# VectorE's scaling of a group of four tiles stands one tile later in the output projection stage

## The chip, the cores and the metric

The kernel runs on one core of a Trainium2 chip. The metric is the time of one execution on the device, in microseconds (us). Three executions of the kernel before gave 2685.3, 2689.87 and 2693.89 us, with the median at 2689.87 us.

## The reference

The reference is one transformer layer on 4096 tokens of width 512, with a context of 3202 rows. Cross attention with 16 heads is followed by a residual addition, then a mixture of 8 experts of which each token uses the best two, then another residual addition:

```python
x = x + _L0_xattn_ref(_layernorm(x), ctx, ctx, Wq, bq, Wk, bk, Wv, bv, Wo, bo)
x = x + _L0_ffn_ref(_layernorm(x), W_experts, b_experts, W_router, b_router)
# in _L0_xattn_ref, at its end:   return out @ Wo + bo
# in _L0_ffn_ref:
router_weights = jax.nn.softmax(jnp.einsum('bsd,ed->bse', x, W_router) + b_router, axis=-1)
topk_w, topk_idx = jax.lax.top_k(router_weights, 2)      # other experts get weight 0
expert_out = jnp.einsum('bsd,eod->bseo', x, W_experts) + b_experts
return jnp.einsum('bseo,bse->bso', expert_out, router_weights)
```

The change touches the part in the middle: `out @ Wo + bo`, the residual sum, the second layernorm's statistics, and the routing.

## The kernel before

The kernel has four stages, each a block of its own: `projections` (q, k, v), `attention` (the bulk of the time), `route_tokens` (the stage that is changed) and `mix_experts`. A stage begins when every engine has ended the one before. Engines run their instructions strictly in the order in which they are written; between engines the order is made by semaphores, all written out by hand.

`route_tokens` (L1172) walks over 32 tiles of 128 tokens, in eight groups of four (`G4 = 4`; below, q is the group and i the step). Per tile it does this:

- TensorE `project(i)` (L1434): 12 matmuls (L1441), attention output times Wo, split in a high and a low part, into one of four PSUM banks.
- VectorE `residual(i)` (L1357): adds x (with the bias, which GpSimd has added in `with_bias`, L1290) into `rows` (L1364), then takes the statistics (L1366).
- At a group's last tile VectorE does `spread(q)` (L1368): mean and variance of four tiles. ScalarE does `root(q)` (L1311): logarithm, then exponential, which gives 1/sqrt(variance), with a table load in front of each. VectorE does `scale(q)` (L1377): five small operations that refine it and write the scale and shift columns of `rows`; the last one raises `rows_ready`.
- ScalarE `normal(i)` (L1317, waits for `rows_ready` of its group), TensorE `turn(i)` (L1444, four transposes, L1449), ScalarE `copy_turned(i)` (L1326), TensorE `route(i)` (L1452, the router's matmuls, L1458).
- Per group VectorE does `choose(q)` (L1386, the two best experts and their counts), ScalarE `exps(q)` (L1332), VectorE `weights(q)` (L1407).

Beside this, each of the 32 steps readies one piece (128x512) of the expert weights: SyncE loads it (`load_piece`, two buffers), ScalarE rounds it (`split_high`, L1309), and VectorE (even pieces) or GpSimd (odd pieces) takes the rest (`split_low`, L1245), after which the buffer may be loaded again. SyncE issues all transfers of the stage: x tiles (`load_x`, ring of three, waits for the residual), attention output (`load_o`, 2 x 512 KB every second tile), pieces, and `store_rows(q)` (L1261), which waits for `rows_ready` and writes 1040 KB.

The order on every engine is set by constants at the head: an operation for tile n stands in step n + constant. Each engine's loop over steps then lists what stands in a step and in which order. In the kernel before, VectorE's step 4q+3 holds the residual of that tile, `spread(q)`, `weights(q-2)` and `scale(q)`; `choose(q-2)` stands in step 4q+2. ScalarE's `root(q)` stands at the end of step 4q+3, `normal(4q)` in step 4q+4. TensorE's `turn(4q)` stands in step 4q+5, behind `project(4q+5)`.

Of the kernel before, what the change touches and what calls it, by code (L numbers as in the profile page):

```python
# [1171 lines left out]
def route_tokens(nc, mem, sb0, sem, psum, ident, g, h):  # L1172
# [3 lines left out]
    NTL, K, table, we_hi, we_lo, picked, before, mix = (h[n] for n in "NTL K table we_hi we_lo picked before mix".split())  # L1176
    lane, number, own, token, rows_stored = (h[n] for n in "lane number own token rows_stored".split())
    G4 = 4
    NGR = NTL // G4
    TURN, ROUTE = 5, 6  # L1180
    NORM = 4
    FIRST_STEP, SECOND_STEP = 10, 11
    STEPS = (NGR - 1) * G4 + SECOND_STEP + 1
    WO_BANKS, T_BANK, R_BANK = 4, 4, 6
    RING = 3
# [1 line left out]
    with mem:  # L1187
# [48 lines left out]
        def piece(n):  # L1236
            return n % KT, n // KT

        def lo_of_piece(eng, n):
            return eng.wait_ge(we_lo_pool, n // 2 + 1) if n % 2 else eng.wait_ge(we_lo_dve, n // 2 + 1)  # L1240

        def split_low(eng, n, done):
            k, e = piece(n)
            eng.wait_ge(we_hi_ready, n + 1)
            eng.tensor_tensor(we_lo[:, k, e, :], we_raw[n % 2][:], we_hi[:, k, e, :].bitcast(F32), ALU.subtract).then_inc(done, 1)  # L1245

        with nc.Block() as block:
            @block.sync
            def _(sp):
                def load_x(i):  # L1250
                    sp.dma_start(xb[i % RING][:], x[i * P:(i + 1) * P, :]).then_inc(x_in[i % RING], 16)

                def load_o(head):
                    for part, src in ((o_hi, oh_d), (o_lo, ol_d)):
                        sp.dma_start(part[head % 2][:].bitcast(F32), src[head].rearrange("p k (u r) -> p k u r", u=2)).then_inc(o_in[head % 2], 16)

                def load_piece(n):
                    k, e = piece(n)
                    sp.dma_start(we_raw[n % 2][:], WeT[k * P:(k + 1) * P, e * D:(e + 1) * D]).then_inc(we_in[n % 2], 16)

                def store_rows(q):  # L1261
                    sp.wait_ge(rows_ready, q + 1)
                    sp.dma_start(table[q * G4 * P:(q + 1) * G4 * P, 0:ROW].rearrange("(u p) c -> p u c", p=P),
                                 rows[q % 2][:]).then_inc(rows_stored[q % 2], 16)

                load_o(0)
                for i in range(RING):
                    load_x(i)
                    if i < 2:
                        load_piece(i)  # L1270
                load_o(1)
                for i in range(NTL):
                    if i % G4 == 0 and i:
                        store_rows(i // G4 - 1)
                    if i % 2 and i // 2 + 2 < HEADS:
                        sp.wait_ge(wo_mm, i + 1)
                        load_o(i // 2 + 2)
                    if i + RING < NTL:
                        sp.wait_ge(y_done, i + 1)
                        load_x(i + RING)  # L1280
                    if i + 2 < NE * KT:
                        lo_of_piece(sp, i)
                        load_piece(i + 2)
                store_rows(NGR - 1)
                for b in range(2):
                    sp.wait_ge(rows_stored[b], 16 * (NGR // 2))
# [17 lines left out]
            @block.scalar  # L1304
            def _(act):
                def split_high(n):
                    k, e = piece(n)
                    act.wait_ge(we_in[n % 2], 16 * (n // 2 + 1))
                    act.activation(we_hi[:, k, e, :], we_raw[n % 2][:], ACT.Copy).then_inc(we_hi_ready, 1)  # L1309

                def root(q):  # L1311
                    act.wait_ge(var_ready, q + 1)
                    act.activation(log_var[:], var[:], ACT.Ln).then_inc(log_ready, 1)
                    act.wait_ge(log_ready, q + 1)
                    act.activation(rstd[:], log_var[:], ACT.Exp, scale=-0.5).then_inc(rstd_ready, 1)

                def normal(i):  # L1317
                    q, u = divmod(i, G4)
                    act.wait_ge(rows_ready, q + 1)
                    if i >= G4:  # L1320
                        act.wait_ge(turned, i - G4 + 1)
                    r = rows[q % 2]
                    act.activation(yn[u][:], r[:, u, 0:D], ACT.Identity, bias=r[:, u, SHIFT_AT:SHIFT_AT + 1],
                                   scale=r[:, u, RSTD_AT:RSTD_AT + 1]).then_inc(yn_done, 1)

                def copy_turned(i):  # L1326
                    act.wait_ge(turned, i + 1)
                    if i >= 2:
                        act.wait_ge(routed, i - 1)
                    act.activation(yT[i % 2][:], psum[:, T_BANK + i % 2, :].rearrange("p (k n) -> p k n", k=KT), ACT.Copy).then_inc(yT_done, 1)  # L1330

                def exps(q):  # L1332
                    act.wait_ge(below_ready, q + 1)
                    act.activation(ex[:], below[:], ACT.Exp).then_inc(ex_ready, 1)

                for i in range(STEPS):
                    if i < NE * KT:
                        split_high(i)
                    if 0 <= i - NORM < NTL:
                        normal(i - NORM)  # L1340
                    if 0 <= i - TURN < NTL:
                        copy_turned(i - TURN)
                    if i < NTL and i % G4 == G4 - 1:
                        root(i // G4)
                    if i >= FIRST_STEP and (i - FIRST_STEP) % G4 == 0:
                        exps((i - FIRST_STEP) // G4)

            @block.vector
            def _(dve):
                n = [0]  # L1350

                def step(ins):
                    n[0] += 1
                    ins.then_inc(chain, 1)
                    dve.wait_ge(chain, n[0])

                def residual(i):  # L1357
                    q, u = divmod(i, G4)
                    dve.wait_ge(wo_mm, i + 1)
                    dve.wait_ge(xb_done, i + 1)  # L1360
                    if u == 0 and q >= 2:
                        dve.wait_ge(rows_stored[q % 2], 16 * (q // 2))
                    row = rows[q % 2][:, u, 0:D]
                    dve.tensor_tensor(row, psum[:, i % WO_BANKS, :], xb[i % RING][:], ALU.add).then_inc(y_done, 1)  # L1364
                    dve.wait_ge(y_done, i + 1)
                    dve.bn_stats(stats[q % 2][:, u, :], row).then_inc(stats_ready, 1)  # L1366

                def spread(q):  # L1368
                    dve.wait_ge(stats_ready, (q + 1) * G4)
                    for u in range(G4):  # L1370
                        ins = dve.bn_aggr(mv[:, u, :], stats[q % 2][:, u, :])
                        n[0] += 1
                        ins.then_inc(chain, 1)
                    dve.wait_ge(chain, n[0])
                    dve.tensor_scalar(var[:], mv[:, :, 1], EPS, None, ALU.add).then_inc(var_ready, 1)

                def scale(q):  # L1377
                    dve.wait_ge(rstd_ready, q + 1)
                    step(dve.tensor_tensor(tmp[:], rstd[:], rstd[:], ALU.mult))
                    step(dve.tensor_tensor(tmp[:], tmp[:], var[:], ALU.mult))  # L1380
                    step(dve.tensor_scalar(tmp[:], tmp[:], -0.5, 1.5, ALU.mult, ALU.add))
                    step(dve.tensor_tensor(rows[q % 2][:, :, RSTD_AT], rstd[:], tmp[:], ALU.mult))
                    dve.scalar_tensor_tensor(out=rows[q % 2][:, :, SHIFT_AT], in0=mv[:, :, 0], scalar=-1.0, in1=rows[q % 2][:, :, RSTD_AT],
                                             op0=ALU.mult, op1=ALU.mult).then_inc(rows_ready, 1)
# [33 lines left out]
                for i in range(STEPS):  # L1418
                    if i < NTL:
                        residual(i)  # L1420
                        if i % 2 == 0:
                            split_low(dve, i, we_lo_dve)
                    if i >= FIRST_STEP and (i - FIRST_STEP) % G4 == 0:
                        choose((i - FIRST_STEP) // G4)
                    if i < NTL and i % G4 == G4 - 1:
                        spread(i // G4)
                    if i >= SECOND_STEP and (i - SECOND_STEP) % G4 == 0:
                        weights((i - SECOND_STEP) // G4)
                    if i < NTL and i % G4 == G4 - 1:
                        scale(i // G4)  # L1430

            @block.tensor
            def _(pe):
# [382 lines left out]
```

## Time and profile before

| | us |
|---|---|
| median of three executions | 2689.87 |
| profiled execution, time | 2697.49 |
| profiled execution, span | 2695.7 |
| TensorE busy in the span | 2560.7 |
| changed stage, from its first transfer to the next stage's first operation | 2212.29 to 2374.76 |

The page gives busy times, shares and the costliest groups of instructions for the one profiled execution. The trace of the same execution can be asked for the instructions of a stretch in order of time, each with the idle time of its engine before it and what ended that idle time, for the waits between engines in a stretch, and for the busy time, TensorE's granted clock (1.00 is 2.4 GHz, 0.50 is 1.2 GHz) and the DMA traffic of a stretch.

### The profile page before, as it was taken

Reading aid. Unit: us, or ns where it says so; the run is one execution under the profiler, and the core shown is the slowest. Engines: PE = TensorE matmul, PEld = TensorE weight load, DVE = VectorE, ACT = ScalarE, POOL = GpSimd, SP = SyncE. Lnnn points to the kernel's source line nnn. Section 1 sums busy time; section 2 is a strip of 40 time slices with the busy share of each in tenths; the row PEclk is TensorE's granted clock in tenths of the full one; section 3 lists DMA queues with packets and bytes.
Section 4 is the critical chain, followed back from the end, with each engine's and each line's share of the span. In section 5 each row is a group of like instructions: output and inputs, shape, how many; then the busy total and the mean of one; then the engine's idle time right before and its main releaser. Section 6 shows DMA issues by size and latency. Waiting matters only on the chain. (4 is left out here: it accounts for less than half of the span.)

```text
span 2695.7 us, 42991 instructions
## 1 busy us (share of the span) xinstructions
PE 2560.7 (95%) x14123; PEld 1286.6 (48%) x14123; DVE 2298.3 (85%) x1810; ACT 1910.6 (71%) x2141; POOL 383.2 (14%) x324
## 2 busy tenths in 40 slices
PE   8999399999999999999999999999999969879998
PEld 7878233333333333333333333333333327768776
DVE  4377399999999999999999999999999966657555
ACT  3123388888888888888888888888888845523333
POOL 2122100000000000000000000000000014315664
PEclk9999699999999999999999999999999989969999
DMA  7446841000051100005110000511000028724463
GB/s 254 160 153 213 189 120 39 22 21 20 21 118 24 37 20 21 21 21 118 25 36 21 20 21 20 118 28 33 21 21 21 21 67 310 250 83 132 126 216 125
DMA packets 125744, 222.77 MB, mean 83 GB/s; under 512 B 19666, under 2 KB 51930, under 8 KB 124772
## 3 DMA queue, kind: packets, MB, share of 16 engines
q1 hardware_dynamic: 110468, 177.57, 23.3%
q0 software_dynamic: 15072, 42.49, 5.0%
q8 instruction: 127, 2.08, 0.3%
q14 instruction: 77, 0.63, 0.1%
HBM read 146.67 MB, written 91.14 MB: 88 GB/s over the span
## 5 line engine op out<-in xcount | busy, mean ns | idle before, releaser
L964 ACT ACTIVATE probs<-psum 128x1024 f32<-128x1024 f32 x1664 | 1612.1, 1024 | 244.4 <-PE psum L1088 215.2
L1017 DVE TENSOR_TENSOR sums<-sums,probs 128x2048 f32<-128x2048 f32 x704 | 1647.3, 2340 | 44.8 <-ACT probs L964 19.4
L1088 PE MATMUL psum<-q_st,k_st 97*128 97x512 f32 x3328 | 1004.8, 423 | 49.5 <-DMA q_st<-shift_scratch 23.6
L1088 PEld LDWEIGHTS psum<-q_st,k_st 97*128 97x128 f32 x3328 | 563.0, 189 | 825.4 <-ACT probs L964 673.7
L1095 PE MATMUL psum<-probs,v_st 128*32 128x512 f32 x6656 | 890.1, 607 | 0.0
L821 POOL TENSOR_TENSOR o_low<-o_sb,o_high 128x512 fp32r<-128x512 f32 x32 | 74.4, 2325 | 1791.3 <-ACT o_high L938 1791.3
L1095 PEld LDWEIGHTS psum<-probs,v_st 128*32 128x32 f32 x6656 | 131.5, 108 | 308.2 <-ACT probs L964 219.1
L1764 PE MATMUL psum<-we_hi,wo 128*128 x624 | 219.7, 414 | 8.5 <-issue 5.8
L1617 ACT ACTIVATE wo<-psum 128x512 fp32r<-128x512 f32 x78 | 46.8, 600 | 138.3 <-PE psum L1750 101.8
L1764 PEld LDWEIGHTS psum<-we_hi,wo 128*128 128x128 f32 x624 | 120.4, 193 | 35.3 <-issue 9.6
L1674 DVE TENSOR_TENSOR res<-psum,be_all 128x512 f32<-128x512 f32 x78 | 53.9, 691 | 93.3 <-PE psum L1764 92.3
L1764 PE MATMUL psum<-we_lo,wo 128*128 x312 | 125.0, 401 | 0.0
L1022 DVE RECIPROCAL recip<-psum 128x512 f32<-128x512 f32 x32 | 107.2, 3350 | 2.1 <-PE psum L1095 2.1
L1610 ACT ACTIVATE xs<-hold 128x512 f32<-128x512 f32 x78 | 63.2, 811 | 64.3 <-DMA hold<-token_rows,near 37.4
L1441 PE MATMUL psum<-wo,att_hi 128*128 128x512 f32 x256 | 85.4, 415 | 17.0 <-DMA att_lo<-ol_scratch 17.0
L336 POOL TENSOR_TENSOR squares<-o_hi 128x512 fp32r<-128x512 f32 (+1 forms) x60 | 60.6, 1019 | 207.2 <-ACT o_hi L374 120.0
L1017 DVE TENSOR_TENSOR sums<-probs 128x2048 f32<-128x2048 f32 x32 | 73.1, 2284 | 11.9 <-ACT probs L964 11.8
L374 ACT ACTIVATE o_hi<-psum,bk_col 128x512 fp32r<-128x512 f32 (+1 forms) x28 | 17.4, 642 | 91.7 <-PE psum L589 91.7
L1095 PE MATMUL psum<-probs,ones 2*32 2x512 f32 (+1 forms) x512 | 67.3, 596 | 0.0
L1680 DVE SCALAR_TENSOR_TENSOR res<-res,w_of,hold 128x512 f32<-128x512 f32 x78 | 58.7, 753 | 9.4 <-DMA hold<-token_rows,far 6.4
L1764 PEld LDWEIGHTS psum<-we_lo,wo 128*128 128x128 f32 x312 | 60.5, 194 | 11.1
L1309 ACT ACTIVATE we_hi<-we_raw 128x512 fp32r<-128x512 f32 x32 | 20.0, 625 | 63.3 <-DMA we_raw<-in_WeT 63.3
(184 smaller groups left out, 1890.6 us busy)
## 6 DMA issues: line engine op xcount, KB each, us to landing
q_st<-qh_scratch SPq DMA_DIRECT2D x64, 256.0 KB
token_rows<-rows SPq DMA_DIRECT2D x8, 1040.0 KB, 5.2
xn<-in_x SPq DMA_DIRECT2D x16, 512.0 KB, 6.6
qh_scratch<-o_hi SPq DMA_DIRECT2D x8, 1024.0 KB, 4.5
ql_scratch<-o_lo SPq DMA_DIRECT2D x8, 1024.0 KB, 7.7
q_st<-ql_scratch SPq DMA_DIRECT2D x32, 256.0 KB
token_rows<-in_x SPq DMA_DIRECT2D x1, 8192.0 KB, 30.4
oh_scratch<-o_high SPq DMA_DIRECT2D x128, 64.0 KB, 1.6
```

What stands on the lines that cost most here:

```text
L336: pool.tensor_tensor(squares[:, j, 0:w], h, h, ALU.mult).then_inc(squared, 1)
L821: pool.tensor_tensor(o_low[:], o_sb[:], o_high[:].bitcast(F32), ALU.subtract).then_inc(low_ready, 1)
L964: nc.scalar.activation(probs[:, p_slot[t], 2 * half:2 * half + 2, :], psum[:, 2 * slot:2 * slot + 2, :], ACT.Exp, scale=SCALE).then_inc(ex ...
L1017: nc.vector.tensor_tensor(sums[b][:], a[:], probs[:, p_slot[t]], ALU.add).then_inc(added, 1)
L1022: nc.vector.reciprocal(recip[:], psum[:, SUM_BANK, :]).then_inc(inverted, 1)
L1088: mm = nc.tensor.matmul(psum[:, 2 * slot + h % 2, :], k_st[:, h, t * P:(t + 1) * P], q_st[:, b, h, :], start=True, stop=True)
L1095: mm = nc.tensor.matmul(psum[h * DH:(h + 1) * DH, bank, :], lhs(h), rhs(h), start=start, stop=stop)
L1441: mm = pe.matmul(psum[:, i % WO_BANKS, :], A[b][:, j, r, :], W[:, j, :], start=t == 0, stop=t == len(terms) - 1)
L1610: act.activation(xs[s % 2], r[:, 0:D], ACT.Identity, bias=r[:, SHIFT_AT:SHIFT_AT + 1], scale=r[:, RSTD_AT:RSTD_AT + 1]).then_inc(xs_done, 1)
L1674: dve.tensor_tensor(res[s % RES][:, 0:D], psum[:, OUT_BANKS[s % 4], :], be_all[:, ds(e, 1), :].rearrange("p o n -> p (o n)"), ALU.add).the ...
L1680: dve.scalar_tensor_tensor(out=res[s % RES][:, 0:D], in0=res[s % RES][:, 0:D], scalar=w_of[k][:, n:n + 1], in1=rest, op0=ALU.mult, op1=ALU ...
L1764: mm = pe.matmul(psum[:, OUT_BANKS[s % 4], :], A[s % 2][:, k, :], W[:, k, ds(e, 1), :].rearrange("p o n -> p (o n)"), start=t == 0, stop=t ...
```

## The change

Every constant from `NORM` on rises by one, so `normal`, `turn`, `copy_turned`, `route`, `choose` and `weights` each stand one step later against `project` and `residual`. `scale(q)` moves from VectorE's step 4q+3 to the end of step 4q+4. ScalarE's `root(q)` moves from the end of step 4q+3 into step 4q+4, behind `split_high(4q+4)` and ahead of `normal(4q-1)` and `copy_turned(4q-2)`. On SyncE `store_rows(q)` moves from the head of step 4q+4 behind that step's `load_x`, still ahead of its `load_piece`. The stage has one step more at its end.

```diff
-    TURN, ROUTE = 5, 6
-    NORM = 4
-    FIRST_STEP, SECOND_STEP = 10, 11
+    NORM, TURN, ROUTE = 5, 6, 7
+    FIRST_STEP, SECOND_STEP = 11, 12
@@ SyncE
                 for i in range(NTL):
-                    if i % G4 == 0 and i:
-                        store_rows(i // G4 - 1)
                     if i % 2 and i // 2 + 2 < HEADS:
                         sp.wait_ge(wo_mm, i + 1)
                         load_o(i // 2 + 2)
                     if i + RING < NTL:
                         sp.wait_ge(y_done, i + 1)
                         load_x(i + RING)
+                    if i % G4 == 0 and i:
+                        store_rows(i // G4 - 1)
                     if i + 2 < NE * KT:
@@ ScalarE
                     if i < NE * KT:
                         split_high(i)
+                    if 0 < i <= NTL and i % G4 == 0:
+                        root(i // G4 - 1)
                     if 0 <= i - NORM < NTL:
                         normal(i - NORM)
                     if 0 <= i - TURN < NTL:
                         copy_turned(i - TURN)
-                    if i < NTL and i % G4 == G4 - 1:
-                        root(i // G4)
@@ VectorE
                     if i >= SECOND_STEP and (i - SECOND_STEP) % G4 == 0:
                         weights((i - SECOND_STEP) // G4)
-                    if i < NTL and i % G4 == G4 - 1:
-                        scale(i // G4)
+                    if 0 < i <= NTL and i % G4 == 0:
+                        scale(i // G4 - 1)
```

## Rows read from the trace of the kernel before

**Rows 1.** The page's head.
```profile
span 2695.7 us, 42991 instructions
```

**Rows 2.** Waits, 2200 to 2400 us: total us, times, longest.
```profile
ACT we_hi L1309 <- DMA we_raw<-in_WeT: 63.3, 17, 14.3
...
PE psum L1449 <- ACT yn L1323: 9.9, 6, 5.1
```

**Rows 3.** Timeline of TensorE: start, duration, operation, count, idle before.
```profile
2238.54 0.66 PE L1449 MATMUL psum<-ident,yn 128*128 128x128 f32 x4 [1.79 <-ACT yn L1323]
...
2280.63 0.60 PE L1449 MATMUL psum<-ident,yn 128*128 128x128 f32 x4
...
2288.89 0.60 PE L1449 MATMUL psum<-ident,yn 128*128 128x128 f32 x4
...
2306.85 0.65 PE L1449 MATMUL psum<-ident,yn 128*128 128x128 f32 x4 [1.11 <-ACT yn L1323]
...
2324.82 0.66 PE L1449 MATMUL psum<-ident,yn 128*128 128x128 f32 x4 [0.98 <-ACT yn L1323]
```

**Rows 4.** Timeline of SyncE's queue, stores of four groups.
```profile
2254.08 0.38 SPq L1263 DMA_DIRECT2D token_rows<-rows  x1
...
2271.32 0.38 SPq L1263 DMA_DIRECT2D token_rows<-rows  x1
...
2287.79 0.38 SPq L1263 DMA_DIRECT2D token_rows<-rows  x1
...
2341.85 0.38 SPq L1263 DMA_DIRECT2D token_rows<-rows  x1
```

**Rows 5.** Timeline of ScalarE, around the root of group 3.
```profile
2281.84 0.63 ACT L1309 ACTIVATE we_hi<-we_raw 128x512 fp32r<-128x512 f32 x1 [1.58 <-DMA we_raw<-in_WeT]
...
2283.68 1.28 ACT L1313 ACT_TABLE_LOAD   x1
2284.97 0.21 ACT L1313 ACTIVATE log_var<-var 128x4 f32<-128x4 f32 x1
...
2286.49 0.21 ACT L1315 ACTIVATE rstd<-log_var 128x4 f32<-128x4 f32 x1
...
2299.83 0.63 ACT L1309 ACTIVATE we_hi<-we_raw 128x512 fp32r<-128x512 f32 x1 [3.07 <-DMA we_raw<-in_WeT]
```

**Rows 6.** Timeline of VectorE, group 3, and one row of group 7.
```profile
2276.70 0.69 DVE L1364 TENSOR_TENSOR rows<-psum,xb 128x512 f32<-128x512 f32 x1 [2.12 <-PE psum L1441]
...
2279.18 0.18 DVE L1388 TENSOR_TENSOR logits<-psum,br_all 128x32 f32<-128x32 f32 x1
...
2281.05 0.80 DVE L1405 TENSOR_TENSOR picked_before<-picked_before,picked 128x16 f32<-128x16 f32 x4
2281.89 0.69 DVE L1364 TENSOR_TENSOR rows<-psum,xb 128x512 f32<-128x512 f32 x1
...
2283.75 0.17 DVE L1375 TENSOR_SCALAR var<-mv 128x4 f32<-128x4 f32 x1
...
2284.26 0.86 DVE L1411 TENSOR_TENSOR mix<-ex,inv 128x8 f32<-128x8 f32 x1
...
2351.50 1.75 DVE L1405 TENSOR_TENSOR picked_before<-picked_before,picked 128x16 f32<-128x16 f32 x4
```

**Rows 7.** Stretches: us, busy PE, PEld, DVE, ACT, POOL, granted clock, DMA share, GB/s.
```profile
2287.00:2288.00 1.00, 1.00 (x6) 0.79 (x5) 0.90 (x5) 0.42 (x2) 0.00 (x0) 1.00 0.10 39
...
2294.00:2295.00 1.00, 1.00 (x7) 0.91 (x7) 0.65 (x1) 0.60 (x2) 1.00 (x1) 1.00 1.02 418
...
2326.00:2331.00 5.00, 5.00 (x20) 3.99 (x20) 1.31 (x3) 1.38 (x3) 3.43 (x3) 0.66 1.02 329
```

**Rows 8.** Timeline of TensorE in the tail of the stage.
```profile
2359.05 1.11 PE L1449 MATMUL psum<-ident,yn 128*128 128x128 f32 x4 [5.06 <-ACT yn L1323]
...
2361.52 1.09 PE L1449 MATMUL psum<-ident,yn 128*128 128x128 f32 x4
...
2367.31 3.42 PE L1458 MATMUL psum<-wr,yT 128*128 128x8 f32 x16
```

## The prediction

> **What bounds the kernel now.** I began with the page's head for the span [rows 1] and then asked only for the changed stage, which lasts some 162 us of it. The waits of that stretch come first, because they bound what can be won: TensorE waits 9.9 us for ScalarE's normalised rows [rows 2], in six waits. The timeline of TensorE places them: 1.79 us at the first turn, 1.11 and 0.98 us at those of groups 4 and 5 [rows 3], 5.06 us in the tail [rows 8]; the two left over share 0.96 us. Between such waits TensorE is full: from the turn at 2280.63 to the one two steps on at 2288.89 are 8.26 us [rows 3], so 16.52 us for a group. The stores of rows show the pace that is really kept: from 2254.08 to 2341.85 are five groups [rows 4], 17.55 us each. The excess over TensorE's own work is 1.03 us a group. About 1.7 us of the five groups' 5.2 is no wait but a slow clock: 0.66 over the 5 us after 2326 [rows 7].
>
> What sets this pace is a loop. I call T the moment at which TensorE comes to the turn in step 4q+3 (2280.63 for group 3 [rows 3]). ScalarE waits for the odd weight piece of that step, which lands at 2281.84, then rounds it, does a normal and a copy, and begins the root at 2283.68 [rows 5]; the store goes out at 2287.79 [rows 4]. That is 5.95 us from landing to store. From the store on the DMA engines are full, 418 GB/s against 39 GB/s just before it [rows 7], and the next late piece lands at 2299.83 [rows 5], 12.04 us after the store; one group earlier it was 10.52 us (2271.32 to 2281.84) [rows 4, 5]. ScalarE's 63.3 us of waiting for pieces [rows 2] are the same loop seen from its side. Landing, root, store, full DMA engines, next landing: 16.5 to 18.0 us around.
>
> **The change, part by part.** No instruction is added or removed.
>
> *Steady groups, VectorE.* `choose` now stands between a group's last residual and its spread. A residual starts 0.2 us after TensorE comes to the turn (2276.70 [rows 6], where the turn was 4.13 us ahead of 2280.63). Choose takes 2.67 us (2279.18 to 2281.85), residual start to variance 2.03 us (2281.89 to 2283.92) [rows 6]. The variance comes at T+0.2+2.67+2.03 = T+4.9; before it was at T+3.3. Logarithm to end of exponential is 1.73 us [rows 5], so the root ends at T+6.65 at the earliest. VectorE meanwhile does the next residual (1.45), a split (0.65) and `weights` (up to 1.3 from 2283.92 to 2285.12 [rows 6], some 0.6 undisturbed): free at T+7.6 to T+8.3. With 0.96 us for the scaling the store leaves at T+8.6 to T+9.3, where it was T+7.16. In itself this costs nothing, since TensorE now wants the group's first turn only in step 4q+6, at T+12.4, and the normal takes 0.8.
>
> *Steady groups, ScalarE.* This is the new danger. The root stands ahead of `normal(4q-1)`, which TensorE wants in step 4q+5, at T+8.26. Let the late piece land at T+a (a is 1.21 in group 3). Then: piece, normal and copy 1.84, exponentials 0.2, the next piece 0.55, root 3.02 (2283.68 to 2286.70 [rows 5]), normal 0.8: ready at T+a+6.4. TensorE waits as soon as a exceeds 1.85. Before, it waited for `normal(4q)` at T+a+5.95+0.8, as soon as a exceeded 1.5. The slack gained is 0.35 us, not a tile's 4.13.
>
> *Steady groups, the loop.* Landing to store grows by the piece and the exponentials that now come first: 5.95+0.75 = 6.7 us. Store to landing shrinks by one x load, which SyncE now sends ahead of the store into the idle stretch (39 GB/s): 0.26 MB at 418 GB/s, 0.63 us. Net +0.1 us on a loop of 17.55. I take 0 for the six groups. The lower end is that the whole excess goes, -5.2 us. The upper end takes 0.75 with no relief from the x load, and about half of one more microsecond where choose is held up (1.75 against 0.80 us for the same four additions [rows 6]): +1.1 a group, +6.6 us. What is late in every case is the piece, so nothing that makes the residual earlier shortens it.
>
> The 1.75 us row has a page beside it: the Trainium skill, "SBUF — State Buffer", section "Who interferes with whom", says that a VectorE instruction with two inputs in SBUF is shut out while a GpSimd instruction that reads SBUF runs. By that rule the move speaks against itself, since choose, with its four such additions, now delays the variance; the steady sum would be +1 us in each group where the two meet and 0 elsewhere. The trace shows both durations for the same four additions, which fits.
>
> *Start.* The first turn waited 1.79 us [rows 3]. It now stands behind one more project of 16.52/4-1.25 = 2.9 us, and its chain grows by about 0.55 us for a piece; but that project needs attention rows whose transfer shares full DMA engines. I take -1.2, between -1.8 and 0.
>
> *Tail.* In the last group T is 2351.32 (2359.05 less the 5.06 us of waiting and the two turn-and-route pairs before it). Turn 28 starts at 2359.05 = T+7.73, and from there the work runs at half the clock: 2.47 us from one turn to the next, the end at 2370.73 [rows 8]. After the change one pair fewer has been done by then, 1.25 us at full clock, so T' = T-1.25. Turn 27 must now wait for the normal behind the root: T'+6.65+0.85 = T+6.25. Its pair costs 2.47 us at half clock, and turn 28 starts at T+8.72. The tail is 1.0 us longer; bounds are -1.25 (pair hidden altogether) and +2.1 (choose held up).
>
> Sum: -1.2+0+1.0 = -0.2 us. The profiled execution took 2697.49 us, 7.6 above the median; the terms are differences within 162 us and pass to the median as they are. Next stage begins with work that waits for this one alone, so all of it counts. 2689.87-0.2 is 2690.
>
> **The rivals.**
>
> *A: the loop opens.* The x load sent earlier and the store sent later level the DMA traffic, a falls below 1.85 in all groups and TensorE never waits. For it: a was 1.21 in one group, and the store before that landing had the shorter 10.52 us. Against: the bytes are the same and DMA is full from store to landing. -1.2-5.2+1.0 = -5.4: 2684.5.
>
> *B: the longer chain wins.* Each turn of the loop takes landing to store 6.7 us and store to landing the full 12.04: 18.7 us, +1.1 a group over 17.55. It decides from a = 1.85 on; group 4 had 2.66 (2299.83 against its T, 16.54 after 2280.63). -1.2+6.6+1.0 = +6.4: 2696.3.
>
> *C: waits bring slow clock.* After the 0.98 us wait the granted clock fell to 0.66 for 5 us [rows 3, 7], which cost 1.7 us (0.34 of 5); after the 1.11 us wait nothing followed. If the new waits did this in each of six groups, five more than now, that is +8.5 on the forecast's sum: 2698.2. The page "TensorE: Matmul & The Clock Gate" of the Trainium skill, section "Why this matters for your kernels", advises against idle gaps between bursts of matmuls since the clock then falls back. The fall in the tail, after 5.06 us, is in line with it; by the rule read loosely, C would be the case.
>
> *D: it does not do what it says.* Scaling behind the residual was meant to free that residual. It starts at T+4.9 instead of T+7.1, but nothing waits for it (four banks, and x is never late): 2690, the same as the forecast.
>
> **How the numbers follow.** Forecast and D together 0.54, A 0.2, B 0.16, C 0.1. A measurement of this kernel tells about 0.3% (8 us) from no change. Its forecast lies within, so do A (-5.4) and the middle of B (+6.4). Slower by more: most of C and the upper part of B, 0.09. Faster by more needs more than every wait of the stage outside the tail, 0.04. Same 0.87. The range takes in A and B and most of C: 2683 to 2698.
>
> **What would show it.** Right: VectorE's scaling some 1.5 to 2 us later against TensorE's turns, waits at the turn in steps 4q+5 (not 4q+6) of 0.5 to 1.5 us in most groups, stores still some 17.5 us apart, the first wait mostly gone, the tail about 1 us longer. Stores 16.5 us apart would show A; 18.5 or more B; granted clock under 1.00 within the groups C. The forecast fails if the late piece does not land 10.5 to 12 us after a store.

## The result: slower by 0.45%, and the profile after

Eight executions of the changed kernel gave a median of 2701.78 us (2698.77 to 2713.57); eight of the kernel before, on the same chip, gave 2691.62 us (2685.3 to 2694.77). The medians differ by 10.2 us; the ratio is 1.0045, 95% interval [1.0028, 1.0062]. The forecast of 2690 us was wrong, and so was its range of 2683 to 2698.

The page's head for the changed kernel:

```profile
span 2698.6 us, 42997 instructions
```

The profiled execution took 2700.43 us. The changed stage ran from 2214.30 us (its first transfer) to 2385.23 us (the next stage's first operation): 170.9 us, where it was 162.5, 8.5 us longer.

The two profiled executions as wholes differ by only 2.9 us (2698.6 against 2695.7). The stretch ahead of the stage was 2.0 us longer in the changed one, and the last stage, whose code is the same, was 7.5 us shorter (313.4 against 320.9 us). Over the fourteen profiled executions of this document the last stage took 313 to 321 us, without relation to the length of the changed stage. So the 8.5 us are of the size of the 10.2 between the medians, but no single profile adds up to them.

First the pace. Timeline of SyncE's queue in the changed kernel (start, duration, operation), the stores of groups 1, 2, 3 and 6, which answer to [rows 4]:

```profile
2257.05 0.38 SPq L1262 DMA_DIRECT2D token_rows<-rows  x1
...
2276.18 0.38 SPq L1262 DMA_DIRECT2D token_rows<-rows  x1
...
2294.53 0.38 SPq L1262 DMA_DIRECT2D token_rows<-rows  x1
...
2350.72 0.38 SPq L1262 DMA_DIRECT2D token_rows<-rows  x1
```

From group 1 to group 6 are 93.67 us, 18.73 us a group instead of 17.55. These five groups hold 5.9 of the 8.5 us. Of the rest, 0.8 lies before the first store, 0.2 and 0.4 in the first and last interval, and 1.2 in the tail.

Then the waits of the changed kernel between 2200 and 2420 us (total us, times, longest), beside [rows 2]:

```profile
ACT we_hi L1308 <- DMA we_raw<-in_WeT: 74.0, 21, 14.3
...
PE psum L1448 <- ACT yn L1322: 13.1, 7, 4.7
...
DVE rows L1363 <- POOL xb L1291: 9.7, 4, 4.0
...
ACT log_var L1312 <- DVE var L1374: 6.5, 5, 1.9
...
DVE tmp L1378 <- ACT rstd L1314: 1.4, 1, 1.4
```

Two of the same waits in the kernel before:

```profile
DVE tmp L1379 <- ACT rstd L1315: 20.2, 8, 4.9
...
ACT log_var L1313 <- DVE var L1375: 2.9, 2, 1.5
```

TensorE waits 13.1 us for normalised rows instead of 9.9. Two waits that have changed say why: ScalarE's root waits longer for the variance (6.5 us, before 2.9), and VectorE, which used to wait 20.2 us for the root, waits 1.4. VectorE has become the last link. The timeline of VectorE in group 2 shows what it does (start, duration, operation, count):

```profile
2266.75 0.17 DVE L1387 TENSOR_TENSOR logits<-psum,br_all 128x32 f32<-128x32 f32 x1
...
2268.15 0.81 DVE L1400 CAST at<-top_at 128x8 f32<-128x8 uint32 x1
2268.99 1.26 DVE L1401 TENSOR_TENSOR picked<-number,at 128x64 f32<-128x64 f32 x1
2270.28 1.78 DVE L1404 TENSOR_TENSOR picked_before<-picked_before,picked 128x16 f32<-128x16 f32 x4
...
2272.52 0.17 DVE L1374 TENSOR_SCALAR var<-mv 128x4 f32<-128x4 f32 x1
```

The timelines of GpSimd and of ScalarE in the same stretch:

```profile
2267.64 1.30 POOL L1244 TENSOR_TENSOR we_lo<-we_raw,we_hi 128x512 fp32r<-128x512 f32 x1 [5.65 <-ACT we_hi L1308]
2268.89 2.52 POOL L1291 TENSOR_TENSOR xb<-xb,bo_all 128x512 f32<-128x512 f32 x2
```

```profile
2266.93 0.63 ACT L1308 ACTIVATE we_hi<-we_raw 128x512 fp32r<-128x512 f32 x1 [2.10 <-DMA we_raw<-in_WeT]
...
2269.57 1.28 ACT L1312 ACT_TABLE_LOAD   x1
2272.72 0.20 ACT L1312 ACTIVATE log_var<-var 128x4 f32<-128x4 f32 x1 [1.88 <-DVE var L1374]
```

The odd piece lands at 2266.93. That sets off three GpSimd operations in a row, 2267.64 to 2271.41: the piece's low part and two bias additions queued behind it. Choose now runs in just that stretch. It takes 5.31 us instead of 2.67: the comparison takes 1.26 us instead of 0.23, the cast 0.81 instead of 0.17, the four additions 1.78 instead of 0.80. Behind it stands `spread`, so the variance comes at 2272.69, the root waits 1.88 us with its table loaded, and the store leaves 9.25 us after the landing instead of the forecast 6.7. The next turn, that of tile 4q-1, whose normalisation stands behind the root on ScalarE, waits, as the timeline of TensorE shows:

```profile
2275.20 0.66 PE L1448 MATMUL psum<-ident,yn 128*128 128x128 f32 x4 [1.57 <-ACT yn L1322]
...
2349.75 0.66 PE L1448 MATMUL psum<-ident,yn 128*128 128x128 f32 x4 [2.01 <-ACT yn L1322]
```

In the five groups from 2 to 6 this turn waited 1.57, 1.13, 0.34, 1.90 and 2.01 us, 6.95 us in all; in the kernel before the first turns of groups 1 to 5 waited 3.04 us in all. TensorE also waited 1.16 us for an attention transfer at 2304.56, in group 4; the kernel before has no such wait behind its first group.

The stage holds a partial control. In group 4 choose ended (2306.21) before GpSimd's burst began (2306.56), took 2.66 us, and the store left 6.86 us after the landing: the forecast's 6.7. The burst met the variance instead and kept the next residual waiting for its bias, as VectorE's timeline shows, but the root had to wait for neither (it was held by the late piece), and `scale` began less than 0.4 us after the root's end:

```profile
2306.66 1.22 DVE L1374 TENSOR_SCALAR var<-mv 128x4 f32<-128x4 f32 x1
...
2309.16 0.69 DVE L1363 TENSOR_TENSOR rows<-psum,xb 128x512 f32<-128x512 f32 x1 [1.29 <-POOL xb L1291]
```

In groups 2, 3, 5 and 6 choose took 5.31, 4.70, 5.65 and 5.81 us, and landing to store 9.25, 7.95, 9.25 and 9.03.

### The profile page after: what moved, and what is told of

Same layout as the page of the kernel before. It is cut to its first block and busy times, and to the rows that moved or that the text cites. A ratio compares the mean times of both kernels' runs of the same rounds, so it can differ in the third digit from the quotient of the medians.

```text
span 2698.6 us, 42997 instructions
## 1 busy us (share of the span) xinstructions
PE 2562.9 (95%) x14123; PEld 1286.8 (48%) x14123; DVE 2303.5 (85%) x1810; ACT 1910.2 (71%) x2141; POOL 380.6 (14%) x324
## 5 line engine op out<-in xcount | busy, mean ns | idle before, releaser
L1763 PEld LDWEIGHTS psum<-we_lo,wo 128*128 128x128 f32 x312 | 59.7, 191 | 10.9
```

What stands on the lines that cost most here:

```text
L1763: mm = pe.matmul(psum[:, OUT_BANKS[s % 4], :], A[s % 2][:, k, :], W[:, k, ds(e, 1), :].rearrange("p o n -> p (o n)"), start=t == 0, stop=t ...
```

## The experiments

"Surplus" below is what VectorE's small operations in the stage (under 0.3 us undisturbed) took beyond their median duration over all runs, summed over those that took at least 0.05 us more. The sums named in the texts recorded before the runs are up to 2 us higher; they rank the kernels alike. "Pace" is the mean distance of the stores of groups 1 to 6. Surplus, pace and stage are read from the one profiled execution of each run; ratios are of timed executions against the kernel before on the same chip. In the two kernels with "small GpSimd" and in the one with "bias on one column" part of the work is left out.

| kernel | surplus | pace | stage | median, us | ratio, 95% interval |
|---|---|---|---|---|---|
| before | 7.0 | 17.55 | 162.5 | 2691.62 | 1 |
| changed | 13.1 | 18.73 | 170.9 | 2701.78 | 1.0045 [1.0028, 1.0062] |
| spread first | 19.6 | 20.66 | 180.5 | 2712.47 | 1.0069 [1.0052, 1.0087] |
| constants only | 17.0 | 19.75 | 178.0 | 2710.24 | 1.0060 [1.0037, 1.0084] |
| order only | 11.1 | 18.51 | 168.9 | 2698.69 | 1.0021 [1.0010, 1.0033] |
| bias on one column | 4.2 | 17.39 | 163.6 | 2697.04 | 1.0012 [1.0000, 1.0025] |
| changed, small GpSimd | 0.0 | 17.58 | 165.4 | 2695.77 | 1.0003 [0.9993, 1.0013] |
| before, small GpSimd | 0.3 | 17.03 | 160.6 | 2693.84 | 0.9999 [0.9990, 1.0009] |
| before, bias ahead | 17.0 | 19.62 | 172.5 | 2706.23 | 1.0045 [1.0031, 1.0059] |
| before, split on VectorE | 13.0 | 19.14 | 171.9 | 2705.72 | 1.0048 [1.0035, 1.0061] |
| before, attention load last | 18.0 | 21.11 | 182.3 | 2713.65 | 1.0066 [1.0053, 1.0079] |
| before, count behind spread | 9.6 | 17.68 | 162.9 | 2695.60 | 1.0002 [0.9993, 1.0012] |
| both | 6.7 | 16.91 | 157.9 | 2693.18 | 0.9993 [0.9983, 1.0004] |
| changed, choose behind scale | 19.4 | 18.19 | 171.6 | 2699.80 | 1.0016 [1.0006, 1.0026] |

The medians of the kernel before beside the three sets of four runs were 2692.73, 2693.02 and 2694.83 us. Over the thirteen kernels the difference in stage length and the difference of the medians agree within 4.1 us: single profiles carry that much.

**Spread first.** The changed kernel with `spread` ahead of `choose`:

```diff
-   if i >= FIRST_STEP and ...: choose(...)
    if i < NTL and i % G4 == G4 - 1: spread(i // G4)
+   if i >= FIRST_STEP and ...: choose(...)
```

> The changed kernel with spread ahead of choose in VectorE's step 4q+3, all else as changed. Theory M (choose ahead of spread, stretched by GpSimd's burst that the late piece sets off, delays the variance and so lengthens the loop): landing to store falls from 8.1 us (mean of groups 1 to 6) to 6.5-6.9, stores stand 17.1-17.6 us apart instead of 18.73, the stage takes 162-165 us instead of 170.9, the time is 2692-2695 us; choose itself still takes some 5 us in most groups. Theory R1 (root ahead of normal(4q-1) on ScalarE is what costs): stores stay 18.4-18.9 us apart and the time stays 2700-2703 us.

It went the other way, 10 us slower still. The root never waited for the variance again, so that wait was mended. But choose then stood ahead of the next residual and of `scale`, and these slid into GpSimd's next burst. VectorE and GpSimd in group 3 of this kernel:

```profile
2286.00 2.80 DVE L1404 TENSOR_TENSOR picked_before<-picked_before,picked 128x16 f32<-128x16 f32 x4
...
2291.18 1.25 DVE L1410 TENSOR_TENSOR mix<-ex,inv 128x8 f32<-128x8 f32 x1
2292.47 1.21 DVE L1378 TENSOR_TENSOR tmp<-rstd 128x4 f32<-128x4 f32 x1
2293.71 1.22 DVE L1379 TENSOR_TENSOR tmp<-tmp,var 128x4 f32<-128x4 f32 x1
```

```profile
2291.14 1.27 POOL L1244 TENSOR_TENSOR we_lo<-we_raw,we_hi 128x512 fp32r<-128x512 f32 x1 [2.79 <-ACT we_hi L1308]
2292.37 2.54 POOL L1291 TENSOR_TENSOR xb<-xb,bo_all 128x512 f32<-128x512 f32 x2
```

Three operations of 0.17 us take 1.2 us each, one for each GpSimd operation beside them, and the store leaves 11.71 us after the landing. My theory in the form "choose ahead of spread" fell. What it had right is the collision; what it had wrong is that only one place is exposed.

**Constants only, order only.** The two halves of the change, each alone. First the constants on the kernel before:

```diff
-    TURN, ROUTE = 5, 6
-    NORM = 4
-    FIRST_STEP, SECOND_STEP = 10, 11
+    NORM, TURN, ROUTE = 5, 6, 7
+    FIRST_STEP, SECOND_STEP = 11, 12
```

> The kernel before with the constants alone raised by one: root stays at the end of ScalarE's step 4q+3, scale in VectorE's step 4q+3, the store at the head of SyncE's step. Choose now stands ahead of spread, but nothing stands between piece 4q+3 and the root. M: the variance is still late, landing to store 7.5-8.5 us, stores 18.2-18.8 us apart, stage 168-171 us, time 2698-2702 us. R1: stores 17.3-17.7 us apart, stage 161-164 us, time 2690-2693 us.

Then the moved root, scale and store with the old constants (the same lines taken back in the changed kernel):

> The changed kernel with the constants of the kernel before (4, 5, 6, 10, 11): only root, scale and the store stand later. Choose is back in step 4q+2, ahead of the residual and not of the spread. M: choose 2.7-3.7 us, landing to store 6.4-6.8 us, stores 17.2-17.8 us apart, stage 162-165 us, time 2690-2694 us. R1: the time is near that of the changed kernel, 2698-2702 us, since root stands just as late on ScalarE.

Constants only: the direction was right, the size short (178.0 us against 168 to 171, and a median of 2710.24 against 2698 to 2702). The root waited 2.3 to 3.1 us for the variance in every group from 2 on. Order only: 168.9 us, above what I expected, and the median of 2698.69 us lies in the range that I had given for the rival R1 (the later root), though choose is back in its old place. In groups 2 to 4 it met nothing, 2.67 us, and landing to store was 6.4 to 7.5 us; in groups 5 and 6 it took 5.73 and 5.86 us, and landing to store rose to 10.26 in both. So each half costs time alone, the constants more than the whole change, and the two do not add up. The rival (the later root as such) does not explain the first half, which leaves the root where it was; in the second half its part and that of the collisions are not separated.

**Bias on one column.** The changed kernel with the collisions thinned:

```diff
-   pool.tensor_tensor(xb[i % RING][:], xb[i % RING][:], bo_all[:], ALU.add)
+   pool.tensor_tensor(xb[i % RING][:, 0:1], xb[i % RING][:, 0:1], bo_all[:, 0:1], ALU.add)
```

> The changed kernel with GpSimd's bias addition cut to one column of 512, so that the output lacks the bias in the other columns: GpSimd's burst beside choose falls from 3.8 us to about 1.5. M with the shared port as the reason of the stretch: choose 2.7-3.7 us instead of 4.7-5.8, landing to store 6.8-7.5 us, stores 17.2-17.8 us apart, stage 163-166 us, time 2692-2696 us. If the stretch has another reason (DMA traffic, for one), choose stays at 4.7-5.8 us and stores at 18.4-18.9 us.

The stage is 163.6 us, choose took 3.3 to 3.8 us in groups 2 to 6, the pace is 17.39; the median is 1 us above the range I gave. The order of all engines is the changed one.

**Small GpSimd, in the changed kernel and in the one before.** To take the collisions away altogether, GpSimd's subtraction on odd pieces also became a write of zeros, which reads nothing; the bias stays on one column:

```diff
+   if done is we_lo_pool:
+       return eng.memset(we_lo[:, k, e, :].bitcast(F32), 0.0).then_inc(done, 1)
```

> The changed kernel with GpSimd's reads cut down: the bias addition on one column of 512, and the low part of the odd weight pieces set to zero instead of computed, so the output lacks both. The theory by now, C (collisions): each small VectorE operation with two inputs in SBUF that meets a GpSimd operation takes about 1 us longer, and the change moved more of them into GpSimd's bursts; over the length of an undisturbed one they had 7.8 us in the kernel before, 14.6 in the changed one, 20.9, 17.5, 13.1 and 4.6 in the four runs so far, whose stages took 162.5, 170.9, 180.5, 178.0, 168.9 and 163.6 us. C: surplus below 2 us, choose 2.7 us in every group, stores 16.6-17.3 us apart, stage 159-163 us, time 2688-2694 us. Rival R4 (the later root on ScalarE costs by itself): stage 166-170 us with choose at 2.7 us.

> The same cut of GpSimd's work (no bias in 511 columns, no low part of odd pieces) in the kernel before. C: surplus below 1 us, and the stage falls from 162.5 to 157-161 us, within 2 us of the same cut in the changed kernel: without collisions the two orders cost the same but for the tail. R4: it stays 5 us or more shorter than the changed kernel with the same cut.

VectorE's four additions of choose as a group in the changed kernel with this cut (count, min/median/max ns), and a GpSimd write in its timeline:

```profile
L1406 DVE TENSOR_TENSOR picked_before<-picked_before,picked x32: 174/174/177, 2268.7 to 2376.1; 128x16 f32<-128x16 f32 x32
```

```profile
2266.62 0.53 POOL L1245 MEMSET we_lo<- 128x512 f32 x1 [9.95 <-ACT we_hi L1310]
```

The longest addition is 177 ns, where the changed kernel has 1215 and the kernel before 1224. In time, the changed order falls from a ratio of 1.0045 to 1.0003, while the same cut moves the kernel before by nothing measurable (0.9999). The collisions are most of the loss. The cut does more than take them away: GpSimd's operations are shorter (0.53 us for 1.30), so the odd pieces' buffers come free sooner, and the waits of VectorE for GpSimd's bias are gone. The changed kernel's trace speaks against these as the cause: of its four waits for the bias three lie before 2254 us and one behind the variance of group 4, none in front of a late variance; and with the cut the store to the next landing got no shorter (10.56 us in groups 2 to 6, against 10.27 in the changed kernel with all its work). What is left between the two orders is 4.8 us of stage, 2 us in the medians: 1.25 in the tail, 1.6 before the first store, and 0.55 a group over five, less 0.8 in the first and last interval; landing to store there is 6.6 to 7.7 us instead of 5.9 to 6.2. The stage of 165.4 us and the median are 2 us above what I allowed, and the two stages are not within 2 us of each other as expected, but nearly the 5 us that I had named for the rival R4. This is the part that collisions do not explain; the landing to store that is longer without any collision points to the later root.

**Two changes of GpSimd's work in the kernel before.** Bias addition one tile ahead of the split, and all splits on VectorE:

```diff
-   for i in range(NTL):
-       with_bias(i)
+   with_bias(0)
+   for i in range(NTL):
+       if i + 1 < NTL: with_bias(i + 1)
        if i % 2: split_low(pool, i, we_lo_pool)
```

> The kernel before, all of its work, with GpSimd's bias addition for tile i+1 ahead of its split of piece i, so that a late odd piece sets off one GpSimd operation instead of three. C: surplus 3-6 us instead of 7.8, stores 17.0-17.4 us apart, stage 159-162 us, time 1 to 3 us under the kernel before. R4, or no part of collisions in the kernel before: same time within 1 us.

```diff
    # VectorE, every step                      # GpSimd
-   if i % 2 == 0: split_low(dve, i, ...)
+   split_low(dve, i, ...)
-                                              if i % 2: split_low(pool, i, ...)
```

> The kernel before, all of its work, with all 32 low parts on VectorE (0.68 us each in place of GpSimd's 1.29), GpSimd keeping the bias additions alone. C: fewer and shorter bursts, surplus 2-5 us, the odd piece's buffer free 0.6 us sooner, stage 158-162 us, time 1 to 4 us under the kernel before. Against it: VectorE waits in order for each late piece ahead of spread; if that weighs more, stage 163-166 us.

Both failed as improvements: 13 us over the kernel before. With the bias ahead, GpSimd's bias additions start when x lands and fall on choose instead of behind it: choose takes 3.6 to 5.9 us, the surplus is 17.0. In the second, GpSimd has fewer operations, yet the surplus rose to 13.0 and choose took 4.6 to 4.9 us in groups 2, 3 and 6. In its groups 4 and 5 choose took 2.68 us, and landing to store was still 7.11 and 6.71 us (before: 6.15 and 5.95): the odd split that VectorE now does in order costs too, as I had named against it. How the 13 us divide was not tested. Both fit the reading that a surplus in front of the store costs time, and neither could I foresee from the order of instructions.

**The attention load and the count.** On SyncE the 1 MB attention load moves behind the weight piece, and on VectorE the last part of choose (cast, comparison, four additions, here `count`) moves behind `spread`:

```diff
-   if i % 2 and i // 2 + 2 < HEADS: ...; load_o(i // 2 + 2)     # ahead of load_x
    if i + 2 < NE * KT: lo_of_piece(sp, i); load_piece(i + 2)
+   if i % 2 and i // 2 + 2 < HEADS: ...; load_o(i // 2 + 2)
```

```diff
    if i < NTL and i % G4 == G4 - 1: spread(i // G4)
    if i >= SECOND_STEP and (i - SECOND_STEP) % G4 == 0:
+       count((i - SECOND_STEP) // G4)
        weights((i - SECOND_STEP) // G4)
```

> The kernel before, all of its work, with SyncE's 1 MB load of attention output behind the step's x load and weight piece instead of ahead of them. It tests the other half of the loop, store to landing (11.3 us mean in the kernel before), by taking 2.6 us of traffic from in front of the late piece. If the loop sets the pace: store to landing 8-10 us, TensorE's waits of groups 1 to 6 mostly gone, stores 16.6-17.2 us apart, stage 157-161 us, time 2 to 5 us under the kernel before. If the collisions alone count, the pace depends on where GpSimd's bursts now fall and may be longer: surplus above 12 us with a stage of 166 us or more.

> The kernel before, all of its work, with the last part of choose (cast, comparison, four additions: 1.25 us undisturbed, and the part in which most collisions fall) moved behind spread, into the 1.7-2.9 us in which VectorE waits for the root. C: collisions there are hidden while they stay under that wait; landing to store 5.9-6.2 us in all groups, stores 17.2-17.7 us apart, stage 160-163 us, time within 2 us of the kernel before. If the additions now meet GpSimd's burst in full (5 us), scale comes late and the stage takes 165-170 us.

> Both edits of the two runs before this one. If each does what its theory says, the chain from landing to store stays near 6 us and store to landing at 8-10 us: stores 16.5-16.9 us apart, stage 156-160 us, time 3 to 6 us under the kernel before. If the collisions decide, as in the first alternative of either run, it is no better than the kernel before.

The load moved alone is the slowest in median (2713.65 us) and in stage, the second outcome I had named; the count moved alone changes nothing measurable, as expected; both together give the shortest stage. The kernel with the load alone, group 3, on VectorE, GpSimd and ScalarE:

```profile
2285.52 3.85 DVE L1405 TENSOR_TENSOR picked_before<-picked_before,picked 128x16 f32<-128x16 f32 x4
...
2291.27 0.17 DVE L1375 TENSOR_SCALAR var<-mv 128x4 f32<-128x4 f32 x1
```

```profile
2285.32 1.30 POOL L1245 TENSOR_TENSOR we_lo<-we_raw,we_hi 128x512 fp32r<-128x512 f32 x1 [3.50 <-ACT we_hi L1309]
2286.58 2.54 POOL L1292 TENSOR_TENSOR xb<-xb,bo_all 128x512 f32<-128x512 f32 x2
```

```profile
2291.47 0.20 ACT L1313 ACTIVATE log_var<-var 128x4 f32<-128x4 f32 x1 [3.29 <-DVE var L1375]
```

Four additions last as long as GpSimd's burst, 3.85 us for 0.80, and end 0.25 us after it; the root waits 3.29 us. The kernel with both edits, the same three views:

```profile
2281.41 0.17 DVE L1375 TENSOR_SCALAR var<-mv 128x4 f32<-128x4 f32 x1
2281.49 1.28 DVE L1402 CAST at<-top_at 128x8 f32<-128x8 uint32 x1
...
2283.07 0.80 DVE L1406 TENSOR_TENSOR picked_before<-picked_before,picked 128x16 f32<-128x16 f32 x4
```

```profile
2278.97 1.29 POOL L1245 TENSOR_TENSOR we_lo<-we_raw,we_hi 128x512 fp32r<-128x512 f32 x1 [2.49 <-ACT we_hi L1309]
2280.22 2.52 POOL L1292 TENSOR_TENSOR xb<-xb,bo_all 128x512 f32<-128x512 f32 x2
```

```profile
2281.83 0.20 ACT L1313 ACTIVATE log_var<-var 128x4 f32<-128x4 f32 x1
```

A collision still happens (the cast, 1.28 us), but behind the variance, beside the root. The pace is 16.91 us against TensorE's own 16.52 [rows 3], store to landing is 9.2 to 10.9 us, and TensorE waits at no turn except in the tail. Landing to store, which I expected near 6 us, was 7.0 to 7.3 in groups 2 to 6. The profiled execution has the shortest stage, 157.9 us, but the timed ratio is 0.9993 with an interval that holds 1, and the medians differ by 1.65 us where I expected 3 to 6: it isn't shown to beat the kernel before.

**Choose behind scale.** In the changed kernel, choose and weights one step later still, choose at the end of VectorE's step 4q+4:

```diff
-    FIRST_STEP, SECOND_STEP = 11, 12
+    FIRST_STEP, SECOND_STEP = 12, 13
@@ VectorE
-                    if i >= FIRST_STEP and (i - FIRST_STEP) % G4 == 0:
-                        choose((i - FIRST_STEP) // G4)
                     if i < NTL and i % G4 == G4 - 1:
                         spread(i // G4)
                     ...
                     if 0 < i <= NTL and i % G4 == 0:
                         scale(i // G4 - 1)
+                    if i >= FIRST_STEP and (i - FIRST_STEP) % G4 == 0:
+                        choose((i - FIRST_STEP) // G4)
```

> The changed kernel with choose (and exps) one step later still and behind scale in VectorE's step 4q+4, so that nothing of choose stands between the group's last residual and the store. C: the variance comes at T+2.3, only the five operations of scale can meet GpSimd in front of the store: landing to store 6.7-7.9 us, surplus in front of the store under 1.2 us a group, stores 17.2-18.0 us apart, stage 164-168 us with a tail 1 to 4 us longer than in the changed kernel, time 2694-2700 us. If instead the later root on ScalarE is what costs, stores stay 18.4 us apart or more.

Inconclusive: pace 18.19 us, above the range; landing to store 6.7 to 9.4 us with one of 10.95, in group 1, where three operations of `scale` took 1.15 to 1.20 us each. The pace leaves that group out; counted from the store of group 0 it is 18.6 us a group, against 18.4 in the changed kernel, and the stage is no shorter (171.6 against 170.9). The median, 2699.80 us, lies at the upper end of what I expected, and the ratio of 1.0016 is below the changed kernel's 1.0045, with 15.1 us of the surplus in the four additions, which here stand behind the store. That a surplus there costs little is in line with the ratio and not shown by the stage.

## Why the prediction was wrong

- **The pace is set by a loop from landing to store to landing.** Right. The store to next landing shrank by 1.0 us (groups 2 to 6: 11.28 to 10.27 us; 0.63 forecast), as the x load went ahead of the store. With load and count both moved it was 9.2 to 9.6 us from group 3 on; with the load moved alone it was 10.7 to 12.9, and why it did not shrink there is open. So the loop describes these kernels; that the landing alone sets their pace no run shows.
- **The step that failed: "Choose takes 2.67 us", and with it "In itself this costs nothing" and the 0 for the steady groups.** Choose was costed at a duration from a place where GpSimd was idle, and moved into the stretch that GpSimd fills. It took 4.7 to 5.8 us in four of five groups. The variance came 7.2 to 8.0 us after T there (T as in the prediction, the turn in step 4q+3), not at T+4.9. The prediction held its chain only against the turn wanted at T+12.4; the turn wanted at T+8.26 waits for a normalisation behind the same root. With 1.75 for the root and 0.8 for the normal, as the prediction has them, that is ready at T+9.7 to T+10.5, an estimate of 1.5 to 2.3 us of waiting; 1.1 to 2.0 were measured. Landing to store in groups 2 to 6 became 8.47 us instead of the forecast 6.7, from 6.27: +2.2 -1.0 = +1.2 us a group, 5.9 over five. The upper bound named this term ("half of one more microsecond where choose is held up") from one row of four additions, 0.95 us; the cast and the comparison collide too, and the whole was 2 to 3 us. That bound also adds up to 1.2 us a group and not 1.1 (0.75 and half of 0.95).
- **Rival B** gave 18.7 us a group, +6.4 us in sum and 2696.3 us. The pace came out at 18.73, but by another cause: B let the landing stay late, and what came was VectorE. It had 0.16.
- **The sentence on the shared port** had the mechanism and did not price it. "+1 us in each group where the two meet" is the cost of one collision; there are three or four, because GpSimd runs three operations in a row after a late piece and each small VectorE operation waits for one.
- **Rival D, "nothing waits for it (four banks, and x is never late)"**: VectorE waited 9.7 us, in four waits, for GpSimd's bias additions, which were queued behind the late piece's split. Before, it had none. Only one of the four lies in groups 2 to 6.
- **Tail +1.0 us**: measured 1.24 (17.83 against 16.59 us from the last store to the next stage). Every run with the raised constants and FIRST_STEP at 11 shows 17.8 to 18.0, every one with the old constants 16.6. Right, in place too: the turn that waited (4.66 us) was turn 27, behind the root.
- **Start -1.2 us**: wrong in sign. The first turn's wait of 1.79 us went, as forecast, but the second turn waited 1.52 us, its normalisation standing behind a piece that landed late (2246.68), and 1.21 us went to the attention transfer, which I had only mentioned (0.29 before). The 0.8 us before the first store are another matter: landing to store grew there from 5.35 to 6.32 us, by the extra piece.
- **Rival C, slow clock**: between the stores of groups 1 and 6 the granted clock was 0.98 before and 1.00 after. Not the cause. After the wait of 2.01 us it was 0.73 for 6.3 us, behind these groups; after those of 1.57 and 1.90 us it stayed at 1.00.
- **The chances**: 0.09 for slower by over 0.3%. The upper ends of the three terms add up to 8.7 us (0, 6.6 and 2.1), which is what the stage lost; the steady groups, taken at 0, stood at their upper end (5.9 us over five groups and 0.6 in the intervals beside them). The median went past this sum by 3.2 us, of which 1.75 lie in the kernel before, whose median of eight executions is that much above the three the forecast started from.

Not settled: how much the stage of one kernel varies from one execution to the next, since each kernel has one profile; by the comparison with the medians a stage length is not safe to better than some 4 us. No run keeps all the work and the changed order and has nothing collide ahead of the store, so how much of the 10.2 us is the collisions' rests on the two kernels with GpSimd's work cut.

## What to carry to other kernels

An instruction's duration belongs to its place: before moving a run of small VectorE operations, lay GpSimd's timeline over the new place, and price every one of them that meets a GpSimd operation which reads SBUF at that operation's length. A moved instruction is not protected by the slack in front of what it used to delay; ask what is queued behind it in its new place (here `spread`, the root, the store and the next weight piece). Small operations that nobody waits for may stand behind the one that somebody waits for, so that a collision falls into an idle stretch; here that took the waits of TensorE out of the steady groups together with the moved load, and no gain in time was shown.

## What the runs showed of the hardware

- A VectorE operation of 0.16 to 0.23 us with two inputs in SBUF took up to 1.2 to 1.4 us beside a GpSimd operation of 1.25 to 1.3 us that reads SBUF; four in a row took 3.85 us beside three of them. The cast (1.28 us) and the variance's scalar operation (1.22 us) were held up in the same way, with a single input.
- Nothing of the kind beside a GpSimd write of zeros: 32 additions of 174 to 177 ns. The residual, which reads one input from PSUM and one from SBUF, was never held up: in the kernel with spread first, whose surplus is 19.6 us, its 32 took 674 to 692 ns. The Trainium skill, "SBUF — State Buffer", section "Who interferes with whom", says the same of both: writes of GpSimd do not contend, nor does a VectorE operation with at most one SBUF input outside the two-port modes.
